# The last two batches written out in one list, filler products in four of TensorE's gaps, gate columns of the last batch apart

## The reference, cut to what matters

```python
c   = x @ cond_weight[id[b]].T                     # 512 x 512, another one for each batch
q, k, v = rope(c @ Wq), rope(c @ Wk), c @ Wv        # 32 heads of 16, 8 groups of keys and values
x1  = x + softmax_causal(q @ k.T / 4) @ v @ Wo
y   = x1 @ W2.T + (x1 @ lora_A[id2[b]]) @ lora_B.T / 2
base, logits, h = y @ W_base.T + b_base, y @ W_router.T, y @ experts_A   # 512, 8 and 8 x 16 columns
w   = softmax of the two largest logits, placed at their experts, 0 elsewhere
out = x1 + base + 2 * (h * w) @ experts_B
```

## Time and profile before

| | us |
|---|---|
| three runs | 278.2, 283.87, 281.39 |
| their median | 281.39 |
| the profiled execution, its own time | 283.47 |
| its span, first to last instruction | 281.7 |
| PE, DVE, ACT, POOL busy in the span | 240.7, 182.8, 117.7, 86.6 |
| mean granted clock of TensorE | 0.936 |

### The profile page before, as it was taken

One profiled execution on the slowest core, in us unless ns is written; L12 is line 12 of the kernel. 1 busy time (PEld: TensorE's weight loads), 2 busy tenths in 40 slices (PEclk: granted clock), 3 DMA queues, 4 the chain that ended last, 5 costly groups with the idle time before them and its releaser, 6 DMA issues.

```text
span 281.7 us, 5626 instructions
## 1 busy us (share of the span) xinstructions
PE 240.7 (85%) x1968; PEld 179.1 (64%) x1968; DVE 182.8 (65%) x908; ACT 117.7 (42%) x269; POOL 86.6 (31%) x92
## 2 busy tenths in 40 slices
PE   0664799999699999999999999999999975985783
PEld 0444589887377866677577658665967753672582
DVE  2682756333983888489748976896689489237324
ACT  2776142557446155614562364436324610540110
POOL 7107314505816052506430662148001300020100
PEclk9967589999899999999999999999999999599778
DMA  5999430050004301520160026002001100110000
GB/s 149 339 330 343 146 97 0 3 186 2 5 9 93 134 1 47 154 72 3 47 219 6 3 64 209 0 3 84 2 0 41 47 2 0 48 40 0 37 0 37
DMA packets 20000, 21.16 MB, mean 75 GB/s; under 512 B 6405, under 2 KB 11525, under 8 KB 19973
## 3 DMA queue, kind: packets, MB, share of 16 engines
q1 hardware_dynamic: 19972, 20.81, 23.4%
HBM read 18.71 MB, written 2.10 MB: 74 GB/s over the span
## 4 chain that ended last, share of the span: by engine, by line
PE 56%; DVE 24%; ACT 8%; issue 8%; SPq 2%; DMA 2%; POOL 0%; DVEq 0%
PE bank L855 8%; PE bank L860 8%; PE bank L856 7%; DVE thrown L622 7%; PE bank L994 3%; PE bank L882 3%; PE bank L928 3%; DVE turned L640 3%; PE bank L866 3%; PE bank L1042 2%; PE bank L942 2%; DVE late L555 2%; PE bank L943 2%; PE bank L944 2%; PE bank L1043 2%
## 5 line engine op out<-in xcount | busy, mean ns | idle before, releaser
L332 POOL TENSOR_TENSOR cond_w_lo<-cond_raw,cond_w_hi 128x512 fp32r<-128x512 f32 x28 | 36.4, 1312 | 71.1 <-ACT cond_w_hi L385 71.1
L622 DVE CUSTOM_DVE_ANT_0 thrown<-bank,causal 128x128 f32<-128x128 f32 x256 | 56.2, 284 | 0.0
L348 POOL TENSOR_TENSOR rope_b<-rope_a,rope_b 128x128 f32<-128x128 f32 (+1 forms) x16 | 16.3, 1016 | 53.2 <-DVE rope_b L674 53.2
L855 PE MATMUL bank<-qkv_w_hi,c_t_hi 128*128 128x512 f32 (+1 forms) x64 | 23.4, 381 | 1.4 <-DVE c_t_lo L555 1.4
L942 PE MATMUL bank<-cond_w_hi,xt_hi 128*128 128x512 f32 x32 | 14.4, 451 | 9.5 <-DVE cond_w_lo L555 9.5
L856 PE MATMUL bank<-qkv_w_lo,c_t_hi 128*128 128x512 f32 (+1 forms) x64 | 22.3, 364 | 0.0
L357 POOL TENSOR_TENSOR x_bias<-x,bias_row 128x512 f32<-128x512 f32 x8 | 10.2, 1278 | 36.4 <-DVE x L712 36.4
L855 PE MATMUL bank<-fused_w_hi,late 128*128 128x324 f32 x64 | 21.1, 339 | 0.0
L622 DVE DVE_READ_ACCUMULATOR2_ANT neg_max<- 128x1 f32 x256 | 20.8, 81 | 0.0
L856 PE MATMUL bank<-fused_w_lo,late 128*128 128x324 f32 x64 | 19.9, 321 | 0.0
L385 ACT ACTIVATE cond_w_hi<-cond_raw 128x512 fp32r<-128x512 f32 x32 | 17.8, 622 | 5.0 <-DMA cond_raw<-cond_w_t 4.9
(11 more groups left out here) (148 smaller groups left out, 632.7 us busy)
## 6 DMA issues: line engine op xcount, KB each, us to landing
cond_raw<-cond_w_t SPq DMA_DIRECT2D x7, 1024.0 KB, 5.6
xt_raw<-x_t SPq DMA_DIRECT2D x8, 256.0 KB, 6.0
x_nat<-x SPq DMA_DIRECT2D x8, 256.0 KB, 2.6
out<-out_sb SPq DMA_DIRECT2D x8, 256.0 KB, 2.0
cond_raw<-cond_w_t SPq DMA_DIRECT2D x4, 256.0 KB, 3.9
stage_a<-w_q SPq DMA_DIRECT2D x4, 256.0 KB, 5.2
stage_b<-w SPq DMA_DIRECT2D x4, 256.0 KB, 4.7
stage_a<-base_t SPq DMA_DIRECT2D x1, 1024.0 KB, 7.4
```

What stands on the lines that cost most here:

```text
L332: pool.tensor_tensor(cond_w.lo[:, k, :], cond_raw[:, k, :], f32(cond_w.hi[:, k, :]), ALU.subtract).then_inc(cond_lo, 1)
L348: pool.tensor_tensor(qk[:, at:at + w], rope_a[:, at:at + w], rope_b[:, at:at + w], ALU.add).then_inc(qk_ready, 1)
L622: nc.vector.tensor_tensor_reduce(thrown[:, p % 2, j, e, :], s_ps[j][:, at:at + P], causal[:, :], -1.0, -MASKED, ALU.add, ALU.min, neg_max[ ...
L855: nc.tensor.matmul(out, lhs.hi[:, k, :], rhs.hi[:, k, cols], start=(k == 0), stop=False)
```

## The change

The loop over rounds ends after round 6 (t = BATCH - 2). What stood in rounds 7, 8 and 9 is written out by hand on every engine behind it, in another order. LAST is batch 7. `project_ffn(5, 1)` is taken out of round 6 and comes in the list behind it. Freed banks are used, so that other waits stand ahead of `context`, `project_out` and `project_ffn`. `keep_busy(n)` issues n matmuls of two constant tiles (bf16, 128 x 384), whose result is read by nobody; there are four places with 6, 12, 5 and 6 of them. For batch 7, half 0 of `project_ffn` is done in two products, first the 136 columns of the gates and then the 188 of the base, and `add_x_base(7)` stands behind `gate_hidden(7)`. The diff, cut to its core (the other hunks put `attn_ps(r)`, `max_ps(t)`, `left_ps`, `base_ps` and `right_ps` in place of the banks' names, and add a wait of `transpose_hidden(5)` for `max_spread` and of `project_low(6)` and `(7)` for `ht_lo`):

```diff
+        ctx_ps = lambda r, e: ((c_ps, s_ps[0]) if r == LAST else (y_ps, c_ps) if r == LAST - 1 else (c_ps, d_ps))[e]
+        attn_ps = lambda r: s_ps[1] if r == LAST else y_ps if r == LAST - 1 else x_ps
+        max_ps = lambda t: d_ps if t == LAST else c_ps
+        left_ps = lambda r: s_ps[2] if r == LAST else c_ps
+        base_ps = lambda r: s_ps[0] if r == LAST else c_ps
+        right_ps = lambda r: s_ps[3] if r == LAST else x_ps
...
-        ROUNDS = range(-1, BATCH + 2)
+        ROUNDS = range(-1, BATCH - 1)
+        LAST = BATCH - 1
...
+            store(LAST - 2)
+            load_batch(LAST)
+            store(LAST - 1)
+            store(LAST)
...
+            for r in (LAST - 1, LAST):
+                split_a(r)
+                add_bias(r)
...
+            exp_top(LAST - 2)
+            spread_maxima(LAST)
+            split_context(LAST - 1)
+            exp_scores(LAST, 0)
+            split_hidden(LAST - 2)
+            exp_scores(LAST, 1)
+            split_x1(LAST - 1)
+            split_low(LAST - 1)
+            split_context(LAST)
+            split_a(LAST)
+            exp_top(LAST - 1)
+            split_hidden(LAST - 1)
+            split_x1(LAST)
+            split_low(LAST)
+            exp_top(LAST)
+            split_hidden(LAST)
...
+            choose_experts(LAST - 2)
+            add_x_base(LAST - 2)
+            maxima(LAST, 0)
+            maxima(LAST, 1)
+            turn_context(LAST - 1, 0)
+            scale_context(LAST - 1, 0)
+            maxima(LAST, 2)
+            maxima(LAST, 3)
+            split_maxima(LAST)
+            turn_context(LAST - 1, 1)
+            scale_context(LAST - 1, 1)
+            turn_back(LAST - 1)
+            gate_hidden(LAST - 2)
+            split_context(LAST - 1)
+            add_x(LAST - 1)
+            split_hidden(LAST - 2)
+            turn_context(LAST, 0)
+            scale_context(LAST, 0)
+            add_out(LAST - 2)
+            split_x1(LAST - 1)
+            turn_context(LAST, 1)
+            scale_context(LAST, 1)
+            turn_back(LAST)
+            split_low(LAST - 1)
+            split_context(LAST)
+            choose_experts(LAST - 1)
+            add_x_base(LAST - 1)
+            gate_hidden(LAST - 1)
+            add_x(LAST)
+            split_hidden(LAST - 1)
+            split_x1(LAST)
+            add_out(LAST - 1)
+            split_low(LAST)
+            choose_experts(LAST)
+            gate_hidden(LAST)
+            dve.wait_ge(base_done, 1)
+            add_x_base(LAST)
+            split_hidden(LAST)
+            add_out(LAST)
...
-                    if r > 0:
+                    if r == LAST:
+                        pe.wait_ge(ctx_turned, 2 * r)
+                    elif r == LAST - 1:
+                        pe.wait_ge(q_lo, BATCH)
+                    elif r > 0:
                         pe.wait_ge(x_base_added, r)
-                elif r > 0:
+                elif r == LAST - 1:
+                    pe.wait_ge(x_base_added, r)
+                elif 0 < r < LAST:
...
-                if r > 0:
+                if r == LAST:
+                    pe.wait_ge(exped, 8 * BATCH)
+                elif r == LAST - 1:
+                    pe.wait_ge(ctx_turned, 2 * r + 1)
+                elif r > 0:
                     pe.wait_ge(out_ready, r)
...
-            def project_ffn(r, n, to):
+            def project_ffn(r, n, to, part=slice(0, HALF)):
+                cols = slice(n * HALF + part.start, n * HALF + part.stop)
                 if r == 0:
                     pe.wait_ge(fused_lo, FUSED)
-                with_high(to[:, 0:HALF], x1_t, fused_w, fused_cols[n])
-                with_low(to[:, 0:HALF], x1_t, fused_w, fused_cols[n], last=False)
+                if n == 1 and r == LAST - 1:
+                    pe.wait_ge(out_ready, r)
+                if n == 0 and r == LAST - 1:
+                    pe.wait_ge(ctx_turned, 2 * r + 3)
+                with_high(to[:, part], x1_t, fused_w, cols)
+                with_low(to[:, part], x1_t, fused_w, cols, last=False)
                 pe.wait_ge(low_lo, r + 1)
-                return nc.tensor.matmul(to[:, 0:HALF], low_t, lora_g[:, fused_cols[n]], start=False, stop=(n == 0))
+                return nc.tensor.matmul(to[:, part], low_t, lora_g[:, cols], start=False, stop=(n == 0))
 
             def transpose_hidden(q):
...
+            def keep_busy(n):
+
+                for _ in range(n):
+                    nc.tensor.matmul(d_ps[:, 0:D - P], ident_b[:, :], later_b[:, 0:PAIRS - 1, :], start=True, stop=True)
...
-                if batch(r):
-                    project_ffn(r, 1, x_ps)
+                if batch(r) and f < LAST:
+                    project_ffn(r, 1, right_ps(r))
+            context(LAST - 1, 0)
+            context(LAST - 1, 1)
+            keep_busy(6)
+            score(LAST, 2)
+            score(LAST, 3)
+            project_ffn(LAST - 2, 1, right_ps(LAST - 2))
+            keep_busy(12)
+            transpose_maxima(LAST)
+            score_t(LAST, 0)
+            project_out(LAST - 1)
+            transpose_hidden(LAST - 2)
+            score_t(LAST, 1)
+            context(LAST, 0)
+            transpose_x1(LAST - 1)
+            finish_ffn(LAST - 2)
+            context(LAST, 1)
+            keep_busy(5)
+            project_low(LAST - 1)
+            project_ffn(LAST - 1, 0, left_ps(LAST - 1)).then_inc(gates_done, 1)
+            project_ffn(LAST - 1, 1, right_ps(LAST - 1))
+            project_out(LAST)
+            transpose_hidden(LAST - 1)
+            transpose_x1(LAST)
+            finish_ffn(LAST - 1)
+            keep_busy(6)
+            project_low(LAST)
+            project_ffn(LAST, 0, left_ps(LAST), slice(0, GATES)).then_inc(gates_done, 1)
+            project_ffn(LAST, 0, base_ps(LAST), slice(GATES, HALF)).then_inc(base_done, 1)
+            project_ffn(LAST, 1, right_ps(LAST))
+            transpose_hidden(LAST)
+            finish_ffn(LAST)
 
 def kernel(x, itok_B_3_7, itok_B_0_2, L0_cond_weight, L0_attn_Wq, L0_attn_Wk, L0_attn_Wv, L0_attn_Wo, L0_attn_cos,
            L0_attn_sin, L0_cond2_W, L0_cond2_lora_A, L0_cond2_lora_B_w, L0_ffn_W_base, L0_ffn_b_base,

```

More of the change, by code:

```diff
@@ L454, in spread_maxima @@
                 for p in range(PER):
[L455 removed]
+                    last = copy(max_rows[:, p, :], max_ps(t)[:, SIDE], own_p[:, p:p + 1])
                 last.then_inc(max_spread, 1)
@@ L639, in turn_context @@
                     dve.wait_ge(ctx_scaled, 2 * r - 1 + e)
-                nc.vector.transpose(turned[e][:, :, :, :].rearrange("q b s d -> q (b s d)"), (c_ps, d_ps)[e][:, :]
+                nc.vector.transpose(turned[e][:, :, :, :].rearrange("q b s d -> q (b s d)"), ctx_ps(r, e)[:, :]
                                     ).then_inc(ctx_turned, 1)
@@ L711, in add_x @@
                     dve.wait_ge(x1b_ready, r)
-                nc.vector.tensor_tensor(x1[:, :], x_ps[:, :], x_nat[:, :], ALU.add).then_inc(x1_ready, 1)
+                nc.vector.tensor_tensor(x1[:, :], attn_ps(r)[:, :], x_nat[:, :], ALU.add).then_inc(x1_ready, 1)
             def split_x1(r):
                 dve.wait_ge(x1t_hi, r + 1)
-                low_of(flat(x1_t.lo), x_ps[:, :], flat(x1_t.hi)).then_inc(x1t_lo, 1)
+                low_of(flat(x1_t.lo), attn_ps(r)[:, :], flat(x1_t.hi)).then_inc(x1t_lo, 1)
             def split_low(r):
@@ L1013, in finish_ffn @@
                 pe.wait_ge(ht_hi, q + 1)
-                for to, cols, first in ((x_ps[:, 0:HALF], slice(LEFT, D), False),
-                                        (x_ps[:, HALF:D], slice(0, LEFT), True)):
+                for to, cols, first in ((right_ps(q)[:, 0:HALF], slice(LEFT, D), False),
+                                        (right_ps(q)[:, HALF:D], slice(0, LEFT), True)):
                     nc.tensor.matmul(to, hidden_t.hi, moe_b.hi[:, cols], start=first, stop=False)
@@ L1103, in _ @@
                     project_low(r)
-                    project_ffn(r, 0, c_ps).then_inc(gates_done, 1)
+                    project_ffn(r, 0, left_ps(r)).then_inc(gates_done, 1)
                 if t >= 0 and batch(f):
```

28 lines of the change are left out of this document (16 added, 12 removed).

## The result

| | before | after |
|---|---|---|
| median | 281.61 us (4 executions, 278.2 to 283.87) | 269.52 us (4, 267.88 to 270.99) |
| profiled execution, its own time | 283.47 us | 269.5 us |
| its span | 281.7 us | 267.7 us |
| mean granted clock | 0.936 | 0.974 |
| from the start of `score(7, 0)` to the end of the span | 55.6 us | 43.3 us |

What follows compares the result with a forecast made beforehand. PE bounds the unchanged front up to some 230 us, dependencies and clock the tail. Span 281.7 - 11.4 = 270.3, plus 1.77 gives 272.1; half of the profile's 2.1 excess off: 271, range 268 to 276.5.

Steps and rivals of the forecast that it cites:

- The maxima's step: Three DVE steps (1.6 + 0.2 + 0.65 us) go behind split_maxima(7), so the transpose of batch 7's maxima starts 2.4 us earlier.
- PE's cover for batch 7's context: Ahead of project_out(7), PE's halves of batch 6 cover DVE's and ACT's path for batch 7's context, 1.9 us to spare.
- the walk: Step-by-step sum along PE's list in the tail, with durations from round 6 at full clock; total gain 11.4 us.
- The gate columns: project_ffn(7) half 0, gates first: 1.55 us gates, 1.7 base; gates 0.5 us earlier, but nothing given back at the end.
- The rule for a product's pace: PE products in project_ffn(7): the rows' 0.115 us for 128 columns taken over 59 ns for 136; 0.12 used.
- Fillers: The 29 constant products on PE at 0.18 us each, 5.2 us in all, 0.3 + 0.2 us on the path.
- The clock: PE's slow stretches at 0.50 behind idle gaps of about 3 us cost 3.3 + 1.7 + 1.7; about 6 us to win.
- case A: Whole tail as summed, 271 us (268.5 to 273.5), longest PE idle about 1.2 us, so no slow stretch; chance 0.67.
- rival B: Clock falls anyway where PE does small tiles and waits, 236.4 to 239.3 and around 256: 272.5 to 274.5; chance 0.16.
- C: PE's fillers cost 0.36 us each, adding 3.2 us together: 274.2; chance 0.08.
- D: Tail bound by DVE, 245 to 250, around batch 7's context; only the clock won: 276.5; chance 0.07.
- E: Slower: fillers on PE's in-order list eat the 11.4 us gain from 0.64 us each on; chance 0.02.

Runs made afterwards that it cites:

- e5: Changed kernel with gate_hidden(5) put back between batch 7's first and second maxima on DVE; median 270.73 us.
- e6: Changed kernel with both contexts of batch 7 put back behind project_ffn(6, 1), and their DVE and ACT steps moved back too; median 277.1 us.
- e3: Changed kernel with half 0 of project_ffn(7) in one product of 324 columns again; median 269.08 us.
- e10: Changed kernel with all its fillers and batch 7's hiddens transposed ahead of the last five products of project_ffn(7, 1); median 268.93 us.
- e7: Changed kernel without the fillers of the third and fourth place, batch 7's hiddens transposed ahead of project_ffn(7, 1)'s last five products; median 273.33 us.
- e2: Kernel before, order untouched, with 18, 17 and 9 fillers in its own three gaps; median 276.62 us, ratio 0.979.
- e1: Changed kernel without its 29 fillers, order kept; median 269.63 us.
- r_no_filler: Changed kernel without any filler, run again with more executions; median 269.76 us, range 268.87 to 276.87.
- r_early_turn: e7 run again on another chip; median 273.43 us, range 267.56 to 275.53.
- e8_context_late_filled: e6 with 17 fillers in the gap ahead of project_out(7); median 275.96 us.

## Why the prediction was right, point by point

271 was forecast, 269.5 came out, within the range of 268 to 276.5 and on the side (faster) that held 0.91. Its steps, each as a distance from the start of `score(7, 0)` (226.11 in the prediction, 224.38 measured):

| step | forecast | measured |
|---|---|---|
| transpose of the maxima | 10.3 | 10.3 |
| `project_out(6)` | 13.2 | 13.1 |
| `add_x(6)` | 16.2 | 16.1 |
| `project_out(7)` | 26.8 | 26.6 |
| `add_x(7)` | 29.8 | 29.6 |
| `project_low(7)` | 33.0 | 32.6 |
| gates at DVE | 35.6 | 35.15 |
| transpose of the hiddens | 39.2 | 38.4 |
| end of the span | 44.2 | 43.3 |

- **The maxima's step** is right, and e5 shows two thirds of it by undoing that part: 1.6 us on DVE for `gate_hidden(5)`. The other two instructions (0.2 and 0.65 us) were put back by no run; that the transpose came at 10.3, as summed, speaks for them.
- **PE's cover for batch 7's context** is right: 1.9 us to spare were forecast, and 2.2 were there (ACT's split ended at 248.66, `project_out(7)` started at 250.96). Undoing it in e6 cost 5.15 us, of which 2.0 are the contexts themselves and 0.5 the way in which the edit undoes it. The expectation of e6 had left out the contexts; the walk has them in its sum, since it lists what PE does one behind the other.
- **The gate columns.** Nearly half of the 0.9 us by which the walk was too long is here. It put 1.55 and 1.7 us for the two parts; the changed kernel did them in 1.46 and 1.48 (257.87, 259.33, 260.81), 0.113 a product at 136 as at 188 columns, and the other half in 1.94 where 2.05 stood. "The split gives nothing back at the end" was wrong by 0.2 us (e3). Since PE and DVE end within 0.45 us of each other there, whatever one takes off the one is stopped by the other (e10).
- **The rule for a product's pace.** The rows' 0.115 us held: 0.113 was measured at 136 columns. The 59 ns that the prediction takes from the Trainium skill (TensorE: Matmul & The Clock Gate, section "Back-to-back issue gap") are given there for an isolated product; for a stream in which each product has its weight load, the same section gives some 81 ns at 128 columns. The trace disagrees with both, with 115 ns at 128 columns and 113 at 136.
- **Fillers** cost 0.163 us each, between the 0.18 taken and the lowest bound. What those of the last two places were to hold up on the path was nothing: without them PE waited as long (e7). The prediction isn't at one with itself here: its section on fillers puts 0.3 and 0.2 us on the path, its walk 0.6 (0.9 less 0.3) and 0.3.
- **The clock** was the part with nearly the right sum and too simple a reason. The shares are near the forecast: 5.5 us clock (e2) for 6, and 6.8 order for 5 to 6. Of the three slow stretches, put at 3.3, 1.7 and 1.7 us, the first was counted too high: between e2 and the kernel before, the way from the maxima's transpose to that of batch 6's x1 differs by 2.5 us, and the other two stretches by 1.6 each. That no gap of 3 us is left was not enough of a reason for case A. Without fillers the new order has no gap above 2.16 us, and yet a slow stretch came in every profile (e1, r_no_filler), in the worst one behind gaps of 0.67 and 0.86 us. What rival B describes thus happens in this order when fillers are missing. That those of the last two places keep it away is borne out for the kernel with the early transpose (e10 against r_early_turn). For the changed kernel, none of whose ten executions was above 271.3 us, it is likely but within chance. The place around 256, where PE waits between small pieces, had been named in B. The Trainium skill (the same page, section "Part 4: PE-mode transpose") says that a transpose doesn't count as busy for the clock in the same way; no run here separates the transposes from the small gaps beside them.
- **The median.** Half of the profile's 2.1 us above the median was taken off, 1.1. What came was 272.1 less 0.9 for the walk and 1.7 for the front, which is the same in both kernels and was that much shorter in the profile after. That second part is luck of the executions and no merit of the sum.
- **What the order is made of.** `gate_hidden(5)` 1.6 (e5), the contexts 5.15 (e6, with the 0.5 of that edit) and the gate columns 0.2 (e3) come to 6.95 us, near the 6.8. Each is undone alone, from the changed kernel, so they need not add up exactly.
- Rivals C, D and E did not occur: fillers at 0.163 us (C), PE without a gap ahead of `project_out(7)` (D), and no execution slower than those of the kernel before (E).

## What to carry to other kernels

When the last iterations of a pipelined loop have only their back left, write them out and interleave them: put the serial path of the newer iteration in front of the dense products of the older one, and everything that nobody waits for behind the path. First fill the idle gaps of the old order with products of constants, as e2 does: that splits what is to be won into clock and order with one run, before anything is rewritten. Judge a filler by the longest of many executions, not by one profile, and keep it short, because at the lower clock it takes longer too (2.54 us for twelve in e5, part of the time at 0.50, instead of 1.95) and can then hold up the path.

## What the runs showed of the hardware

- Products of fp32r operands with 136 and with 188 columns both start 0.11 us apart at 2.4 GHz (1.46 us for 13 of 136, 1.48 for 13 of 188), so doing the 324 columns of a half in two parts takes 2.94 us instead of 1.94.
- A bf16 product of 128 x 384 takes 0.163 us in a row (24 in 3.90).
- The granted clock was seen to fall behind a stretch in which PE was not idle for more than 0.9 us at a time, and then stayed at 0.50 through 10 us of dense products (259.4 to 269.8 in r_no_filler). In e1_no_filler, the same kernel, the profile has 1.00 there, and ten of the twelve executions of the two were short. So one profile doesn't show it.
- The same gap of 1.44 us behind the same list of PE was followed by 1.00 in e6_context_late and by 0.50 in e8_context_late_filled.
- The mean clock from 10 to 40 us, where all kernels here do the same, was 0.72 in one profile (r_no_filler) and 0.89 in another (r_early_turn), and batch 7's scores start 4.2 us apart in these two.
